# Reading two bias tables back in the other order on the one DMA queue of a relative-position attention

## The reference

```python
c2p_att = jnp.einsum('bhqd,hpd->bhqp', q, pos_k)
c2p = jnp.take_along_axis(c2p_att, c2p_pos, axis=-1)      # by q - k, clipped to buckets
p2c_att = jnp.einsum('bhkd,hpd->bhkp', k, pos_k)
p2c = jnp.swapaxes(jnp.take_along_axis(p2c_att, p2c_pos, axis=-1), -1, -2)
scores = scores + (c2p + p2c) / scale
probs = jax.nn.softmax(scores, axis=-1)
ctx = jnp.einsum('bhqk,bhkd->bhqd', probs, v)
```

## Time and profile before

| | us |
|---|---|
| median of three runs (2779.13 to 2786.41) | 2785.15 |
| the profiled execution | 2782.47 |
| its span in the trace | 2780.7 |

### The profile page before, as it was taken

The page is one execution under the profiler, slowest core; times in us unless marked ns, Lnnn a source line. Parts: engine busy times, 40 slices in busy tenths (PEclk is TensorE's granted clock), DMA queues, the critical chain, the costliest instruction groups (busy, mean ns, idle before and its releaser), DMA issues. The chain is left out here.

```text
span 2780.7 us, 47508 instructions
## 1 busy us (share of the span) xinstructions
PE 1955.3 (70%) x13556; PEld 1434.2 (52%) x13557; DVE 1682.0 (60%) x4293; ACT 1044.3 (38%) x2096; POOL 897.2 (32%) x1080
## 2 busy tenths in 40 slices
PE   6867777777777777778278889665246059999752
PEld 3436665665566565666245656343135018877421
DVE  8846665666666665666466664388747754444343
ACT  3445555555555555555113232332011063333000
POOL 3122222222222222222312120166740005554655
PEclk9969998889999999999679999787565559999975
DMA  5689999989999999999512100000001314447333
GB/s 155 202 237 281 282 288 270 285 264 287 282 275 284 274 287 267 288 289 276 154 31 61 44 17 1 21 0 0 0 1 63 121 75 143 155 150 141 111 101 102
DMA packets 289273, 456.41 MB, mean 164 GB/s; under 512 B 38608, under 2 KB 224000, under 8 KB 289056
## 3 DMA queue, kind: packets, MB, share of 16 engines
q1 hardware_dynamic: 268304, 397.73, 47.8%
q0 software_dynamic: 16592, 43.44, 6.2%
q10 hardware_dynamic: 4160, 12.58, 1.2%
HBM read 236.67 MB, written 216.92 MB: 163 GB/s over the span
## 5 line engine op out<-in xcount | busy, mean ns | idle before, releaser
L890 DVE CUSTOM_DVE_ANT_0 probs<-bank,c2p 128x512 f32<-128x512 f32 x512 | 351.9, 687 | 407.3 <-PE bank L787 208.9
L848 ACT ACTIVATE probs<-probs,neg_max 128x512 f32<-128x512 f32 x512 | 371.4, 725 | 70.6 <-DVE neg_max L890 70.2
L863 ACT COPY a_stage<-bank 128x320 f32<-128x320 f32 (+1 forms) x512 | 211.9, 414 | 406.2 <-PE bank L756 395.4
L899 DVE COPY probsT<-bank 128x512 f32<-128x512 f32 x512 | 351.3, 686 | 10.9 <-PE bank L797 10.6
L797 PE MATMUL bank<-ident,probs 128*128 128x128 f32 x2048 | 332.8, 288 | 1.0 <-ACT probs L848 0.9
L768 PE MATMUL bank<-tab,k 96*128 96x320 bf16 (+1 forms) x512 | 162.8, 318 | 200.1 <-DVE b_stage L842 153.7
L797 PEld LDWEIGHTS bank<-ident,probs 128*128 128x128 f32 x2048 | 274.5, 151 | 12.2 <-issue 1.8
L733 POOL COPY end_c2p<-a_stage 128x4 f32<-128x4 f32 (+1 forms) x128 | 24.9, 194 | 741.1 <-ACT a_stage L863 590.6
L2091 POOL DMA_INDIRECT p_x_tile<-y_d,p_token x160 | 153.0, 956 | 329.9 <-POOLq L1782 207.8
L787 PE MATMUL bank<-ident,p2c 128*128 128x128 f32 x1280 | 244.6, 292 | 0.0
L782 PE MATMUL bank<-k,q 96*128 96x384 bf16 (+1 forms) x512 | 164.9, 322 | 89.6 <-DMA p2c<-p2c_d 57.3
(11 more groups left out here) (252 smaller groups left out, 3830.1 us busy)
## 6 DMA issues: line engine op xcount, KB each, us to landing
p2c_d<-b_stage SPq DMA_DIRECT2D x64, 640.0 KB, 5.0
c2p_d<-a_stage SPq DMA_DIRECT2D x64, 640.0 KB, 4.2
p2c_d<-b_stage SPq DMA_DIRECT2D x64, 576.0 KB, 5.4
c2p_d<-a_stage SPq DMA_DIRECT2D x64, 576.0 KB, 4.2
p2c<-p2c_d SPq DMA_DIRECT2D x256, 144.0 KB, 4.5
c2p<-c2p_d SPq DMA_DIRECT2D x256, 144.0 KB, 3.8
o_sorted_d<-p_o_pair SPq DMA_DIRECT2D x80, 256.0 KB
k<-k_stack_d SPq DMA_DIRECT2D x192, 64.0 KB
```

The costliest lines, as they stand in the source:

```text
L848: act.activation(probs[:, w % 2, j, :], probs[:, w % 2, j, :], ACT.Exp, bias=neg_max[:, w % 2, j:j + 1], scale=-1.0).then_inc(exp_done, 1)
L863: act.copy(staged(a_stage, wa % 2, wa % TPB)[:, j, :], bank[A_BANK][:, 0:width(wa % TPB)]).then_inc(a_copied, 1)
L890: dve.tensor_tensor_reduce(probs[:, w % 2, j, :], bank[S_BANKS[(HB * w + j) % 3]][:], c2p[:, w % 2, j, :], -SCALE, LOWEST, ALU.add, ALU.mi ...
L899: dve.tensor_copy(probsT[:, wp % 2, j], bank[T_BANKS[j % 2]][:].rearrange("p (k q) -> p k q", k=TPB)).then_inc(probsT_copied, 1)
```

## The change

In every step, the c2p reads of unit n + 1, with their waits, stand ahead of the p2c reads of unit n + 2. Nothing else moves: the same DMAs, the same waits, the same destinations, and the other four engines have the same instructions in the same order.

```diff
                         (i2, w2), (i1, w1) = ahead(i, w, 2), ahead(i, w, 1)
+                        if is_unit(i1, w1):
+                            t = w1 % TPB
+                            sp.wait_ge(a_written[w1 % 2], 16 * (BODY // 2 * i1 + w1 // 2 + 1))
+                            apart(sp)
+                            sp.wait_ge(c2p_filled, BODY * i1 + w1 + 1)
+                            read_skewed(c2p_d, w1 % 4, t, c2p[:, w1 % 2], (t - 1) * P, c2p_loaded[w1 % 2])
                         if is_unit(i2, w2):
                             kt = w2 % TPB
                             sp.wait_ge(b_written[w2 % 2], 16 * (BODY // 2 * i2 + w2 // 2 + 1))
                             apart(sp)
                             sp.wait_ge(p2c_filled, BODY * i2 + w2 + 1)
                             read_skewed(p2c_d, kt, kt, p2c[:, kt], 0, p2c_loaded[kt])
-                        if is_unit(i1, w1):
-                            t = w1 % TPB
-                            sp.wait_ge(a_written[w1 % 2], 16 * (BODY // 2 * i1 + w1 // 2 + 1))
-                            apart(sp)
-                            sp.wait_ge(c2p_filled, BODY * i1 + w1 + 1)
-                            read_skewed(c2p_d, w1 % 4, t, c2p[:, w1 % 2], (t - 1) * P, c2p_loaded[w1 % 2])
```

## The result

| | before | after |
|---|---|---|
| median of the runs, us | 2782.14 | 2831.65 |
| lowest to highest, us | 2764.91 to 2786.41 | 2824.77 to 2835.52 |
| ratio, 95% interval | | 1.0187, 1.0138 to 1.0236 |
| profiled execution, span, us | 2780.7 | 2833.8 |

The change made the kernel slower by 1.9% (the ratio compares the means of the runs); the medians are 49.5 us apart. The forecast was a kernel slower by 28 us, with a median of 2813.

The account below looks back on a forecast made before the run. The attention stage was taken as held by transfers or engines waiting for them. Mean shift of both rings, 28 us, plus nothing for SP's fill wait, on 2782.5 gave 2810.5, median 2813; range 2765 to 2860.

Parts of the forecast that it names:

- What bounds the kernel: Attention stage: held by transfers or engines waiting for them, DMA share 0.95; c2p lands last, about 1.0 us late.
- The shifts of the first adds: Attention stage: first adds move by +0.9, +0.9, +0.9 and -1.0 us over four units, as p2c now lands last.
- The gain in every fourth unit: Units with t = 3, needing no new p2c: c2p landing first starts the add 1.0 us earlier.
- the odd ring: Units with t = 1 and 3, each feeding the unit two steps on: collects 0.9 - 1.0, nothing.
- SP's wait for the other fill: SP starts reads 0.2, 1.3, 1.2 and 0 us later, behind POOL's c2p fill; costed at nothing, 43 us if uncovered.
- the cover: While SP waits for the fill, DMA engines still have the two writes just issued, 1.2 MB, so the wait costs nothing.
- The two rings: Attention stage: each unit feeds the one two steps on; even and odd units share the pace, 0.225 x 126 = 28 us.
- the upper branch: Attention stage: the even units alone set the pace, 0.45 x 126 = 57 us.
- the backlog: DMA queue, share 1.06: an engine that waits longer finds the queue shorter, which can give back part of a delay.
- the even ring: Units with t = 0 and 2, each feeding the unit two steps on: collects 1.8 us in four steps, 0.45 a step.

Follow-up runs that it names:

- run of t = 2 alone: Kernel before, with c2p reads ahead of p2c reads only in the steps with t = 2; ratio 1.0014 to the kernel before.
- run of all but t = 2: Kernel before, with c2p reads first in the steps with t = 0, 1 and 3, old order with t = 2; ratio 1.0182.
- two ways of making the fills earlier: Changed kernel with POOL's c2p fill ahead of its p2c fill, 1.0114; or with both fills at the end of the step before, 1.0140.
- SP's early wait alone: Kernel before, reads in old order, but SP waits for the c2p fill already ahead of the p2c reads; ratio 1.0089, 24 us slower.
- the fills early: Changed kernel with both POOL fills at the end of the step before, ahead of copying table b's ends; 1.0140. Kernel before with them: 0.9996.
- the halves: Kernel before with c2p first only with t = 1 and 3, 1.0169, or t = 0 and 2, 1.0047; with early POOL fills 1.0125 and 1.0032.
- odd units' kernel: Kernel before, with c2p reads first only in the steps with t = 0 and 2; ratio 1.0047, with early POOL fills 1.0032.

## Why the prediction was right, and where its sizes were off

**What bounds the kernel: right in kind.** The stage is held by engines that wait for single reads, with a DMA share near 1. That the bytes alone don't set it is shown: the same bytes took 50 us more at a share of 0.88.

**The shifts of the first adds: right.** The forecast had the c2p wait vanish (0.5 us left), PE's p2c wait grow to 150 us or more (209.0), PE's wait for DVE at L768 shrink (148.7 to 29.3 us), and adds start about 1 us behind their scores. All four came. The mean time from a unit's first score to its first add over the stage is 1.30, 1.06, 1.23 and 0.97 us for t = 0 to 3, against 1.75, 2.08, 2.30 and 2.53 before. The forecast's 1.02 us thus holds for the odd units; the even ones, whose scores come behind the long waits, take 0.2 to 0.3 us more, which it hadn't. (In unit 73, from which it took the 1.02, DVE was busy with a copy until the add, so the price was read from the right kind of row but not from a pure one.)

**The gain in every fourth unit: arrives, is worth nothing.** The forecast took 1.0 us for units with t = 3, and that is what the table shows (8.54 to 7.51). In its sum this gain cancels the loss of the odd ring. The run of t = 2 alone and the run of all but t = 2 show that none of it that could be measured reaches the end: the next unit waits for a read whose issue didn't move with the early add.

**SP's wait for the other fill: the step that failed.** "I cost it at nothing", since the DMA engines would still have the two writes. The length of the wait was forecast well (2.7 us in four steps; 93.4 us over the stage, about 0.7 a step), its price was not: alone it costs 24 us of the 43 that the forecast gave as the most, and in the changed kernel some 13 to 20 of its 49 us, by the two ways of making the fills earlier, each with a wide interval. The rows show where the cover ends. Here SP's write of table b is issued by 660.95 and its reads start at 663.12, behind the fill; the stretch of the wait, and the 2 us behind it (the last two numbers are the DMA share and GB/s):

```profile
661.00:663.10 2.10, 1.79 (x27) 1.40 (x29) 2.10 (x7) 2.00 (x5) 2.09 (x3) 1.00 1.02 415
663.10:665.10 2.00, 2.00 (x37) 1.73 (x30) 1.10 (x2) 0.70 (x3) 0.00 (x0) 1.00 0.87 274
```

I took the same over all 69 waits from the packets in the trace. While SP waits, the share is 1.01: the transfers of the writes are there, as the forecast had it. But in the first microsecond behind the start of a step's reads, as a mean over some 120 steps, it is 0.98 before, 0.91 with SP's early wait alone and 0.90 in the changed kernel; with the fills early it is 0.97. I read this as a queue that is full while SP waits, and short just behind, because the writes are through before the late reads have filled it again. The cost is measured; this way from the wait to the cost is argued from the shares and was not tested by itself.

The Trainium skill, on the page "DMA: Bandwidth & Descriptors", section "Issuing engines are not separate DMA queues", says that the time to initiate a DMA is usually small relative to the DMA. Here it isn't: four c2p reads that stand second take 1.78 us to issue, about 0.45 each, and 144 KB at 281 GB/s are 0.5 us. The forecast had said that by this rule the fill wait would cost nothing; alone it cost 24 us.

**The two rings: a size that is not settled, and came near partly by luck.** With the early fills the order costs 1.40%, 38 us, against the 28 predicted and the 57 of the upper branch. In that kernel 36.4 us of SP's wait are left. If a quarter of them is paid, the order costs 29 us; if the queue covers them, as its share of 0.97 suggests, 38. The 28 was built with the gain of every fourth unit in the odd ring. Without it, since it is worth nothing, that ring collects 0.9 us in four steps, 0.225 a step, and the same mean of the two rings gives 0.34 x 126 = 43 us. So the loss taken over was too high, or the backlog gave some of it back, and the counted gain made up for it. The table can't tell the rings apart: from one even unit to the next it has +1.27 us (t = 3 and 0 together, 18.16 to 19.43) and +0.81 (t = 1 and 2, 17.81 to 18.62), where the forecast had 0.9 for each, but by odd units the same four steps add up to the same 2.08 us, with the fill wait in it. In the halves the even units bear most of the order's cost, between 0.7 and 0.8 of it.

**What stays open.** PE's clock. In the changed kernel PE's granted clock is 0.86 in the stage, against 0.91, and the score matmul behind the idle 5.63 us takes 0.39 us where the one of unit 55 took 0.27. Slower matmuls just where everything waits may cost something. The odd units' kernel gives a hold on how much. Its stage:

```profile
170.00:1310.00 1140.00, 877.19 (x8880) 699.95 (x8881) 705.78 (x1690) 598.99 (x1239) 299.44 (x624) 0.86 0.92 274
```

Its clock is the 0.86 of the changed kernel, and it is only 13 us slower than the kernel before; with early fills it has 0.87 and is 9 us slower. So a fall of the clock to this level need not cost more than some 10 us, unless that order gains elsewhere what the clock takes. No run separates the clock from the later reads in the even units, so a part of the 38 us may be clock.

Open too is whether the even ring alone sets the pace (theory D) or each late p2c read costs alike (theory E).

## What to carry to other kernels

A view of waits names the last thing to arrive, not the thing that is late by itself. Before a read is moved ahead, count how long the engine would have been held anyway (here 1.02 of 2 us), and ask what the read that it overtakes releases: here it was the earlier consumer in the chain, whose work stands between the two arrivals, and it had to be served first.

A gain in one step counts only if the next wait depends on it. In a software pipeline with one issuing queue, follow the ring: from a landing over the engines to the issue of the read that is waited for next. Here a step that ended early, ahead of a queue that issues in turn and had its list full, gained nothing.

A wait that is moved ahead on an issuing queue can have a price even if the DMA engines are busy while it lasts. Test it alone: it took one added wait to find 24 us. The DMA share has to be read in the stretch behind the wait (0.91 here), not only in the wait (1.01).

## What the runs showed of the hardware

The group of reads that stands directly behind the two big writes is slow to issue, whichever it is. As means over 200 to 1300 us, four p2c reads take 2.88 us there before and the c2p reads behind them 2.00; in the changed kernel four c2p reads take 2.49 us there and the p2c reads behind them 2.02. Single groups scatter (1.79 to 3.19 us for the first before). In the kernel whose reads stand ahead of the writes, the first group takes 1.87 us. And a share of 0.95 on the DMA engines did not mean that the stage was as long as its transfers. The same transfers ran at shares from 0.79 to 0.95, with a time that differed by 5%, by the order in which they were issued and the waits ahead of them.
